# Two input transfers on another queue and the first product begun earlier: the window stage of a fused graph-network kernel

## The chip, the cores and the metric

One core of a Trainium2 chip. The time is the device time of one execution in microseconds; the median of the runs is compared.

## What is computed

`x` has 1,024 nodes of 512 values, and 16,384 edges (`src`, `dst`, sorted by `dst`) join them. Four layers follow each other, each ending in `x = layernorm(x + layer(x))`. Only the first matters here:

```python
h = x @ W + b
adj = zeros((N, N)); adj[row, col] = 1; adj[col, row] = 1
adj = adj + eye(N)
adj = adj / maximum(adj.sum(1), 1)
out = dw[0] * h; cur = h
for i in range(3):
    cur = adj @ cur
    out = out + dw[i + 1] * cur
return relu(out)
```

The other three layers are a sum over edges with a linear layer, a mean over edges, and graph attention. They use the same matrix C of edge counts (1,024 x 1,024), which the kernel builds once from the edges.

## The kernel before

**Building C.** The sorted edges are taken in 32 quads of 512 edges. For each quad three engines work together. VectorE (`key_hots`) compares keys with a row of numbers and so makes the one-hots of the destination, for each of 8 blocks of source nodes times a window of destination nodes (3 of them in quad 0, 41 in quad 31, so 24 to 328 columns). The one-hots of the source (`hot_lo`) come from ScalarE for quads 2, 4, ... 14 and most of those from 17 on (`distances`, four squares, then `lo_hots`, one Relu), and from VectorE for the others. TensorE (`quad`) multiplies both, two windows of two matmuls each, into PSUM. VectorE (`add_window`) adds each window into `c32`, the matrix C, which must have been zeroed. VectorE's program runs three quads ahead (`LOOK`), so in iteration q it adds the windows of quad q and makes the one-hots of quad q + 3.

**Preparation.** SyncE issues the transfers, the edges first. VectorE computes keys and bounds; ScalarE copies `f_lo`; TensorE turns `f_lo` and `f_key` into columns. ScalarE zeroes tiles of C, `ZERO_ACT` of the eight in parts, GpSimd those up to `ZERO_POOL`, VectorE the rest. Products of a zero tile (`warm`) stand between TensorE's first steps.

**h.** The product x @ W0 is cut into 32 parts, four for each of 8 tiles of nodes; a part (`h_part`, line 852) is one float32 matmul of 512 columns that the trace records as two. `h_parts(q)` says which parts follow quad q, in proportion to each quad's work, from quad 2 to quad 28. When a tile's four parts are done, ScalarE (`h_upper`) evicts it in two activations and VectorE (`h_lower`) takes the low half. Both stand in the engines' programs a fixed number of quads behind `h_quad(t)`, the quad after which tile t is complete. Ahead of the third tile's first part TensorE waits for `far_in`, a flag that VectorE reads in iteration 7 from the PSUM bank that this tile will write.

**Order by hand.** Each engine's program is a fixed sequence; semaphores join them. TensorE waits for W0 and the first piece of x after quad 2. Behind the last quad come the turned blocks of C (line 928) and the adjacency products (lines 976, 991, 1001, 1010), and the other layers.

Of the kernel before, what the change touches and what calls it, by code (L numbers as in the profile page):

```python
# [26 lines left out]
P = 128  # L27
# [18 lines left out]
KEYS = NT * (NQ - 1 + (NQ - 1) // 4 + WIN0)  # L46
RING = 5
LOOK = 3
H_FROM = 2
H_TO = 29  # L50
LO_TURN = 16
WARM = (9, 3, 6, 3)
FILL_FROM, FILL = 29, (1, 6)
COLUMNS_AT = {28: (0,), 29: (1,), 30: (2,)}
H_BANKS = (2, 3, 4, 5, 2, 3, 4, 5)
XT_NODES = ((0, P), (P, HALF), (HALF, N))
ZERO_ACT, ZERO_POOL = 5, 6
F_LO_AFTER = 2
KEYS0 = 144
LEFT_GROUP = 48  # L60
# [48 lines left out]
def window(q):  # L109
    return q + q // 4 + WIN0  # L110
# [6 lines left out]
def build(nc, x, xT, src, dst, W0, b0, dw, W1T, b1, wc, wn, b2, W3, W3T, b3, b3T, aw, ab, out):  # L117
    with ExitStack() as ctx:
# [174 lines left out]
        def by_chunk(t):  # L293
            return t.rearrange("p (c g) -> p g c", c=NC)
# [11 lines left out]
            return H_BANKS[t]  # L306

        def h_parts(q):
            def upto(i):
                return NT * KT * sum(27 + window(j) for j in range(H_FROM, i)) // sum(  # L310
                    27 + window(j) for j in range(H_FROM, H_TO))

            return range(upto(q), upto(q + 1)) if H_FROM <= q < H_TO else ()

        def h_quad(t):
            return min(q for q in range(NQ) if KT * t + KT - 1 in h_parts(q))
# [9 lines left out]
        @block.sync  # L326
        def _(sp):
            sp.dma_start(e_dst, dst.rearrange("(g e) -> g e", e=GROUP)).then_inc(S["edges"], 16)
            sp.dma_start(e_src, src.rearrange("(g e) -> g e", e=GROUP)).then_inc(S["edges"], 16)
            sp.dma_start(first_i[:, 0, :], dst.rearrange("(a g e) -> a g e", a=1, e=GROUP)[:, :, 0],  # L330
                         allow_slow_non_contiguous=True).then_inc(S["edges"], 16)
            sp.dma_start(dwb[:], dw.rearrange("(a d) -> a d", a=1).broadcast_to([P, STEPS + 1])).then_inc(S["dw_in"], 16)
            sp.dma_start(w0raw, W0.rearrange("(k p) n -> p k n", p=P)).then_inc(S["w_in0"], 16)
            for i, (n0, n1) in enumerate(XT_NODES):
                sp.dma_start(xT32[:, :, n0:n1], xT.rearrange("(k p) n -> p k n", p=P)[:, :, n0:n1]).then_inc(S[f"xT_in{i}"], 16)
            sp.dma_start(w3t, W3T.rearrange("(k p) n -> p k n", p=P)).then_inc(S["w_in5"], 16)
            sp.dma_start(xcur[:], x.rearrange("(t p) d -> p t d", p=P)).then_inc(S["x_in"], 16)
            sp.dma_start(b0w, b0.rearrange("(a d) -> a d", a=1).broadcast_to([P, D])).then_inc(S["small_in"], 16)
            for i, b in enumerate((b1, b2, b3)):
                sp.dma_start(bb[:, i, :], b.rearrange("(a d) -> a d", a=1).broadcast_to([P, D])).then_inc(S["small_in"], 16)  # L340
            sp.dma_start(wbc[:], b3T).then_inc(S["small_in"], 16)
            sp.dma_start(abb[:], ab.rearrange("(a h) -> a h", a=1).broadcast_to([P, H])).then_inc(S["small_in"], 16)
            sp.dma_start(abc[:], ab.rearrange("(h a) -> h a", a=1)).then_inc(S["small_in"], 16)

            sp.wait_ge(S["const_ready"], 5)
            step = VCOL + H + 2
            flat = abT[:].rearrange("p k c -> p (k c)")
            for q in range(2):
                for u in range(2):
                    c0 = VCOL * u + q  # L350
                    sp.dma_start(flat[q * DH:(q + 1) * DH, c0:c0 + 3 * step + 1:step],
                                 aw.rearrange("(j q) (u p) -> q u p j", q=2, p=DH)[q, u],
                                 allow_slow_non_contiguous=True).then_inc(S["small_in"], 16)

            sp.wait_ge(S["h_done"], NT)
            for n, w in enumerate((W1T, wc, wn, W3)):
                if n >= 2:
                    sp.wait_ge(S["w_lo"], n - 1)
                sp.dma_start(stage[:, n % 2], w.rearrange("(k p) n -> p k n", p=P)).then_inc(S[f"w_in{n + 1}"], 16)
            for layer in range(1, 3):  # L360
                for t in range(NT):
                    name = ("xT_even", "xT_odd")[t % 2]
                    n = (layer - 1) * NT + t
                    sp.wait_ge(S["x_lo"], layer * NT + t + 1)
                    if n >= 2:
                        sp.wait_ge(S[name], n // 2 * TURNED)
                    for v in range(2):
                        sp.dma_start(xTs[:, v, :, t * P:(t + 1) * P], cur[:, 1, v, t, :],
                                     transpose=True).then_inc(S[name], 16)
            sp.wait_ge(S["uT_in"], 1)  # L370
            sp.dma_start(u_rows.rearrange("h (t p) -> (h t) p", p=P), uT).then_inc(S["u_kept"], 16)
            sp.wait_ge(S["u_kept"], 16)
            sp.wait_ge(S["wx_done"], NT)
            for h in range(2):
                sp.dma_start(uf[:, h], u_rows[h:h + 1].broadcast_to([P, N])).then_inc(S[f"uf_in{h}"], 16)
            for t in OUT_ORDER:
                if t in NORM_ACT:
                    sp.wait_ge(S["out_act"], NORM_ACT.index(t) + 1)
                else:
                    sp.wait_ge(S["out_dve"], NORM_DVE.index(t) + 1)  # L380
                sp.dma_start(out.rearrange("(t p) d -> t p d", p=P)[t], xcur[:, t, :]).then_inc(S["out_done"], 16)
            sp.wait_ge(S["out_done"], 16 * NT)
# [99 lines left out]
        def _(act):  # L482
            def copy(o, i, scale=1.0, **kw):
                return act.activation(o, i, ACT.Copy, scale=scale, **kw)  # L484

            act.sem_inc(S["wx_in"], 2)
            act.sem_inc(S["nv_in"], 2)
            act.wait_ge(S["cols"], 3)
# [5 lines left out]
            zeros(0, F_LO_AFTER)  # L494
            act.wait_ge(S["prep"], LO_IN)
            copy(f_lo, i_lo).then_inc(S["f_lo_in"], 1)
            zeros(F_LO_AFTER, 2 * F_LO_AFTER)

            def split_hi(n, name, raw):
                act.wait_ge(S[f"w_in{n}"], 16)  # L500
# [2 lines left out]
                copy(ws[:, SLOT[name], 0], raw).then_inc(S["w_hi"], 1)  # L503

            act.wait_ge(S["tr"], 1)
            act.activation(lo16[:], by_chunk(ps[:, 2, 0:E // P]), ACT.Copy, bias=1.0).then_inc(S["nslo_in"], 1)
            copy(nslo[:], by_chunk(ps[:, 2, 0:E // P]), -1.0).then_inc(S["nslo_in"], 1)
            act.wait_ge(S["nslo_in"], 2)
            act.wait_ge(S["const_ready"], 4)
            mine = [q for q in range(NQ) if lo_by_act(q)]  # L510
# [18 lines left out]
                copy(cur[:, 0, 0, t, :], ps[:, h_bank(t), :]).then_inc(S["h_hi"], 1)  # L529
                copy(acc[:, t, :], ps[:, h_bank(t), :], dwb[:, 0:1]).then_inc(S["acc0"], 1)  # L530

            def constants():

                for k0, k1 in ((KEYS0, 2 * KEYS0), (2 * KEYS0, KEYS)):
                    act.activation(iota_rep[:, k0:k1, :], iota_rep[:, 0:k1 - k0, :], ACT.Copy, bias=float(k0)).then_inc(S["keys_late"], 1)
                copy(id16[:], id32[:]).then_inc(S["const16"], 1)
                copy(sel[:], id32[0:H, 0:H + 1].unsqueeze(2).broadcast_to([H, H + 1, P])).then_inc(S["const16"], 1)

            tiles_up = 0
            act.wait_ge(S["dw_in"], 16)  # L540
            distances(0)
            zeros(2 * F_LO_AFTER, ZERO_ACT)
            for i, q in enumerate(mine):
                if i + 1 < len(mine):
                    distances(i + 1)
                lo_hots(i)
                if i == 2:
                    constants()
                if mine[i - 1] <= FAR_QUAD < q:
                    act.wait_ge(S["tr"], 3)  # L550
                    act.activation(far, by_chunk(ps[:, 5, 0:E // P]), ACT.Copy, bias=-1.0).then_inc(S["far_in"], 1)
# [3 lines left out]

            for t in range(tiles_up, NT - 1):
                h_upper(t)

            def cast_left(j):
                copy(cst[:, j:j + 2, 0:HALF], c32[:, j:j + 2, 0:HALF]).then_inc(S["cst_left"], 1)  # L560
# [232 lines left out]
        def _(pe):  # L793
# [21 lines left out]
            def warm(n):  # L815

                for _ in range(n):
                    mm(ps[:, 4, :], blank[:, 0:P], blank, start=True, stop=True)

            pe.wait_ge(S["blank_in"], 1)  # L820
            warm(WARM[0])
            pe.wait_ge(S["const_ready"], 4)
            pe.wait_ge(S["f_lo_in"], 1)
            for c in range(NC):
                ins = pe.transpose(ps[:, 2, c * NG:(c + 1) * NG], f_lo[:, c * P:(c + 1) * P], id32[0:NG, 0:NG])
            ins.then_inc(S["tr"], 1)
            warm(WARM[1])
            pe.wait_ge(S["prep"], F_KEY_IN)
            for c in range(NC):
                ins = pe.transpose(ps[:, 3, c * NG:(c + 1) * NG], f_key[:, c * P:(c + 1) * P], id32[0:NG, 0:NG])  # L830
            ins.then_inc(S["tr"], 1)
            warm(WARM[2])

# [44 lines left out]
                        fill(FILL[0])  # L878

            def far_columns():  # L880
                pe.wait_ge(S["idx_far"], 2)
                for c in range(NC):
                    pe.transpose(ps[:, 5, c * NG:(c + 1) * NG], f_far[:, c * P:(c + 1) * P], id32[0:NG, 0:NG])
# [14 lines left out]
            def attention_bias():  # L898
# [4 lines left out]
                ins = mm(ps[:, 3, 264:264 + H], one[:].broadcast_to([P, P]), wba[:, 0, :], start=True, stop=True)  # L903
                ins.then_inc(S["wa_done"], 1)

            for q in range(NQ):
                if q == FILL_FROM:
                    pe.wait_ge(S["acc0"], 5)
                    pe.wait_ge(S["h_lo"], 5)
                quad(q)  # L910
                if q < H_FROM:
                    warm(WARM[3])
                if q == H_FROM:
                    pe.wait_ge(S["key_in"], 1)
                    pe.wait_ge(S["nslo_in"], 2)
                    pe.wait_ge(S["xT_in0"], 16)
                    pe.wait_ge(S["w_in0"], 16)
                if q == FAR_QUAD:
                    far_columns()
                for n in h_parts(q):  # L920
# [362 lines left out]
        def _(dve):  # L1283
# [45 lines left out]
            dve.wait_ge(S["first_in"], 3)  # L1329
            tt(pack, pack, trio[:, :, 1], ALU.bitwise_or).then_inc(S["first_in"], 1)  # L1330
            dve.wait_ge(S["tr"], 2)
            dve.tensor_copy(key16[:], by_chunk(ps[:, 3, 0:E // P])).then_inc(S["key_in"], 1)
            dve.wait_ge(S["first_in"], 5)
            ts(pack, pack, 10, None, ALU.logical_shift_left).then_inc(S["first_in"], 1)
            dve.wait_ge(S["const_ready"], 4)
# [43 lines left out]
            key_hots(1, 1)  # L1379
            lo_hots(1)  # L1380
            key_hots(2, 0)
            dve.wait_ge(S["c32z"], 5)
            tiles_low = 0
            key_hots(2, 1)
            for q in range(NQ):
# [536 lines left out]
```

## Time and profile before

| | |
|---|---|
| median of 3 runs | 385.77 us (385.58 to 386.03) |
| the profiled execution | 385.64 us |
| its span, first to last instruction | 383.8 us |
| TensorE's mean granted clock in it | 0.989 of full |
| TensorE busy | 369.2 us |
| VectorE busy | 277.8 us |
| ScalarE busy | 235.4 us |
| GpSimd busy | 100.3 us |

The first three rows tell how a time read from the trace stands to the measured ones: the span leaves out 1.84 us of its own execution. Busy times are sums over the whole span and overlap.

### The profile page before, as it was taken

To read this page: it belongs to the slowest core of one execution; us is meant where nothing else is said; L and a number is where in the kernel's file an instruction comes from. 1 tells how busy PE (TensorE), PEld (TensorE's weight loads), DVE (VectorE), ACT (ScalarE), POOL (GpSimd) and SP (SyncE) were. 2 spreads that over 40 slices of the span, in tenths; PEclk is the share of its full clock that TensorE was granted. 3 is DMA by queue.
4 is the path that set the end of the run, shared out by engine and by line. 5 is a ranking of instruction groups with operands and counts; after the bars stand their busy time and mean duration, and the time that the engine had idled before them with its cause. 6 is when DMAs were issued, how large, how long until landed. Compare 5 with 4: busy or idle time off the path is not lost.

```text
span 383.8 us, 7745 instructions
## 1 busy us (share of the span) xinstructions
PE 369.2 (96%) x2740; PEld 217.3 (57%) x2740; DVE 277.8 (72%) x608; ACT 235.4 (61%) x402; POOL 100.3 (26%) x91
## 2 busy tenths in 40 slices
PE   8799999999999999999999999999999999999980
PEld 3355585444444444444444444444568889999980
DVE  8799988469986772226755445553995979999994
ACT  8999866678512444222651111477877999999234
POOL 3003000098700477000990000466300000121210
PEclk9999999999999999999999999999999999999995
DMA  5970060032000000000442000133203113110005
GB/s 163 385 236 0 3 207 14 2 127 92 2 0 0 1 2 3 0 2 1 86 94 41 0 0 2 27 80 73 41 2 115 56 55 113 56 57 3 2 3 222
DMA packets 27974, 22.70 MB, mean 59 GB/s; under 512 B 19552, under 2 KB 20768, under 8 KB 27936
## 3 DMA queue, kind: packets, MB, share of 16 engines
q1 hardware_dynamic: 27072, 19.06, 16.9%
q10 hardware_dynamic: 864, 3.15, 2.3%
q8 instruction: 23, 0.38, 0.4%
q14 instruction: 15, 0.12, 0.1%
HBM read 15.87 MB, written 2.13 MB: 47 GB/s over the span
## 4 chain that ended last, share of the span: by engine, by line
PE 87%; DVE 5%; ACT 5%; issue 2%; DVEq 0%; POOL 0%; POOLq 0%
PE ps L805 22%; PE ps L1205 10%; PE ps L1146 8%; PE ps L1047 7%; PE ps L1088 7%; PE ps L1010 7%; PE ps L1001 7%; PE ps L852 6%; PE ps L976 4%; PE ps L991 4%; PE ps L873 3%; ACT cts L516 2%; DVE early L1775 1%; ACT xcur L727 1%; PE ps L893 1%
## 5 line engine op out<-in xcount | busy, mean ns | idle before, releaser
L805 PE MATMUL ps<-big,xTs 128*128 128x512 f16 x384 | 84.3, 379 | 0.0
L805 PEld LDWEIGHTS ps<-big,xTs 128*128 128x128 f16 (+1 forms) x384 | 37.0, 98 | 43.5
L713 ACT ACTIVATE big<-big,uvt 128x1024 bf16<-128x1024 f32 x55 | 58.8, 1147 | 0.0
L614 ACT ACTIVATE big<-xcur,nmr,rstd (+1 forms) x24 | 19.5, 814 | 33.9 <-DVE nmr L1491 33.9
L445 POOL TENSOR_TENSOR big<-xcur,big x16 | 18.5, 1156 | 60.2 <-ACT xcur L615 59.2
L852 PE MATMUL ps<-big,xTs 128*128 128x512 f32 x64 | 32.6, 606 | 0.0
L462 POOL TENSOR_TENSOR xcur<-xcur,c 128x512 f32<-128x512 f32 (+2 forms) x8 | 8.8, 1104 | 87.7 <-DVE c L1694 83.1
L484 ACT ACTIVATE big<-ps 128x512 f16<-128x512 f32 (+1 forms) x16 | 9.4, 587 | 33.3 <-PE ps L805 30.9
L1146 PE MATMUL ps<-big,cst 128*128 128x260 f16 x256 | 29.8, 275 | 0.0
L415 POOL TENSOR_TENSOR big<-xTs,big 128x2048 f16<-128x2048 f32 x4 | 16.2, 4080 | 44.8 <-ACT big L484 44.8
L1010 PE MATMUL ps<-big,adj 128*128 128x512 f16 x128 | 27.9, 379 | 0.0
L1047 PE MATMUL ps<-cst,big 128*128 128x512 f16 x128 | 27.8, 379 | 0.1
L1001 PE MATMUL ps<-big,adj 128*128 128x512 f16 x128 | 27.8, 379 | 0.0
L1088 PE MATMUL ps<-big,cts 128*128 128x512 f16 x128 | 27.8, 379 | 0.0
L1146 PEld LDWEIGHTS ps<-big,cst 128*128 128x128 f16 x256 | 24.3, 96 | 4.8
L1361 DVE TENSOR_TENSOR c<-c,ps 128x24 f32 (+31 forms) x64 | 21.3, 333 | 3.3 <-PE ps L873 3.1
L453 POOL TENSOR_TENSOR big<-xcur,big 128x512 f16<-128x512 f32 x8 | 9.3, 1158 | 51.9 <-ACT xcur L615 51.9
L1344 DVE TENSOR_TENSOR adj<-adj,early 128x48 f16<-128x48 f16 (+31 forms) x64 | 21.7, 341 | 0.4 <-issue 0.2
L873 PEld LDWEIGHTS ps<-adj,cts 128*128 128x128 f16 x128 | 11.1, 107 | 18.2 <-issue 12.1
L1047 PEld LDWEIGHTS ps<-cst,big 128*128 128x128 f16 x128 | 12.4, 98 | 15.4 <-issue 0.6
L1088 PEld LDWEIGHTS ps<-big,cts 128*128 (+1 forms) x128 | 12.5, 98 | 15.1
L1001 PEld LDWEIGHTS ps<-big,adj 128*128 128x128 f16 x128 | 12.5, 98 | 15.1
(226 smaller groups left out, 713.8 us busy)
## 6 DMA issues: line engine op xcount, KB each, us to landing
big<-u_rows ACTq DMA_DIRECT2D x6, 512.0 KB, 3.7
xcur<-in_x SPq DMA_DIRECT2D x1, 2048.0 KB, 17.2
out<-xcur SPq DMA_DIRECT2D x8, 256.0 KB, 2.3
big<-in_W SPq DMA_DIRECT2D x1, 1024.0 KB, 6.0
xTs<-in_xT SPq DMA_DIRECT2D x1, 1024.0 KB, 10.1
big<-in_W3T SPq DMA_DIRECT2D x1, 1024.0 KB, 12.9
xTs<-in_W1T SPq DMA_DIRECT2D x1, 1024.0 KB, 5.5
xTs<-in_wc SPq DMA_DIRECT2D x1, 1024.0 KB, 8.3
```

The source lines that it names most:

```text
L713: act.activation(above[:, a % AHEAD, :], uf[:, h % 2], ACT.Relu, scale=BIG, bias=vb[:, j, h:h + 1]).then_inc(S["above_in"], 1)
L805: return mm(bank, lhs(k)[a], rhs(k)[b], start=start and k == 0 and n == 0, stop=stop and k == KT - 1 and n == 2)
L852: ins = mm(bank, xT32[:, k, t * P:(t + 1) * P], w0raw[:, k, :], start=k == 0, stop=k == KT - 1)
L873: ins = mm(ps[:, WINDOW_BANKS[w % 4], 0:n], left, hot_key[:, r, w % 2 * NC * n:(w % 2 + 1) * NC * n].rearrange("p (k c) -> p k c", c=NC)[: ...
L1001: ins = mm(ps[:, t, :], adj[:, j, t * P:(t + 1) * P], cur[:, 1, v, j, :], start=n == 0 and v == 0, stop=n == NT - 1 and v == 1)
L1010: ins = mm(ps[:, t, :], adj[:, j, bass.ds(t * P, P)], cur[:, 0, v, j, :], start=n == 0 and v == 0, stop=n == NT - 1 and v == 1)
L1047: ins = mm(ps[:, half * KT + k, :], cur[:, 1, v, j, k * P:(k + 1) * P], c[:, j, half * HALF:(half + 1) * HALF], start=c is cst and j == 0 ...
L1088: ins = mm(ps[:, t, :], c[:, j, bass.ds(t * P, P)], cur[:, 0, v, j, :], start=c is cts and j == 0 and v == 0, stop=c is parts[-1] and j == ...
L1146: ins = mm(ps[:, DENSE_BANK[i], 0:4 * (DH + 1)], cst[:, j, t * P:(t + 1) * P], yh[:, j, v, 4 * half:4 * half + 4, DH + 1:YW], start=j == 0 ...
L1205: ins = mm(o, cz[h % CZ][:, j, t * P:(t + 1) * P], yh[:, j, v, h, :], start=j == 0 and v == 0, stop=j == NT - 1 and v == 1)
L1344: tt(hot_key[:, q % RING, w * NC * n:(w + 1) * NC * n].rearrange("p (k c) -> p k c", c=NC), iota_rep[:, 0:n, 0:NC], spread(key16[:], q, n) ...
L1361: added = tt(cells, cells, ps[:, WINDOW_BANKS[w % 4], 0:NT * m].rearrange("p (a w) -> p a w", w=m), ALU.add)
```

## The change

- W0 and the first 128 nodes of the turned x are issued by ScalarE, as the first things it does, no longer by SyncE.
- TensorE waits for both ahead of quad 0, and parts 0 and 1 of h stand there; part 2 follows quad 0, part 3 quad 1. The remaining 28 are spread over quads 2 to 28. The warm-up products behind quads 0 and 1 are gone, and those ahead of quad 0 are one instead of six.
- ScalarE zeroes four tiles of C instead of five, GpSimd two instead of one.
- ScalarE makes the one-hot of its first quad straight behind its squares, and fills the late part of `iota_rep` where it did before, but `id16` and `sel` only behind all h tiles save the last.
- The banks of the turned columns move (2 and 3 to 4 and 5), the warm-up's from 4 to 3, and the waits that guarded them move to where the banks are used again.

```diff
-H_FROM = 2
+H_FIRST, H_FROM = {-1: (0, 1), 0: (2,), 1: (3,)}, 2
-WARM = (9, 3, 6, 3)
+WARM = (9, 3, 1)
-ZERO_ACT, ZERO_POOL = 5, 6
+ZERO_ACT, ZERO_POOL = 4, 6
...
         def h_parts(q):
+            if q in H_FIRST:
+                return H_FIRST[q]
...
-                return NT * KT * sum(27 + window(j) for j in range(H_FROM, i)) // sum(
+                return KT + (NT - 1) * KT * sum(27 + window(j) for j in range(H_FROM, i)) // sum(
                     27 + window(j) for j in range(H_FROM, H_TO))
...
-            sp.dma_start(w0raw, W0.rearrange("(k p) n -> p k n", p=P)).then_inc(S["w_in0"], 16)
-            for i, (n0, n1) in enumerate(XT_NODES):
+            for i, (n0, n1) in enumerate(XT_NODES[1:], 1):
...
+            act.dma_start(w0raw, W0.rearrange("(k p) n -> p k n", p=P)).then_inc(S["w_in0"], 16)
+            act.dma_start(xT32[:, :, 0:P], xT.rearrange("(k p) n -> p k n", p=P)[:, :, 0:P]).then_inc(S["xT_in0"], 16)
...
             act.wait_ge(S["dw_in"], 16)
             distances(0)
-            zeros(2 * F_LO_AFTER, ZERO_ACT)
+            lo_hots(0)
+            distances(1)
             for i, q in enumerate(mine):
-                if i + 1 < len(mine):
+                if 0 < i < len(mine) - 1:
                     distances(i + 1)
-                lo_hots(i)
+                if i:
+                    lo_hots(i)
                 if i == 2:
-                    constants()
+                    keys_late()
...
             for t in range(tiles_up, NT - 1):
                 h_upper(t)
+
+            constants()
...
             def far_columns():
+                pe.wait_ge(S["nslo_in"], 2)
+                pe.wait_ge(S["key_in"], 1)
                 pe.wait_ge(S["idx_far"], 2)
...
+            pe.wait_ge(S["w_in0"], 16)
+            pe.wait_ge(S["xT_in0"], 16)
+            for n in h_parts(-1):
+                h_part(0, n)
             for q in range(NQ):
...
                 quad(q)
-                if q < H_FROM:
-                    warm(WARM[3])
-                if q == H_FROM:
-                    pe.wait_ge(S["key_in"], 1)
-                    pe.wait_ge(S["nslo_in"], 2)
-                    pe.wait_ge(S["xT_in0"], 16)
-                    pe.wait_ge(S["w_in0"], 16)
...
-            dve.wait_ge(S["c32z"], 5)
+            dve.wait_ge(S["c32z"], 4)
```

By `h_parts` 8 parts stand ahead of quad 8 after the change and 5 before; h tile 0 is complete behind quad 1 instead of quad 6, tile 2 begins behind quad 8 instead of quad 11.

## Rows read from the trace of the kernel before

**Rows 1.** The page: busy time, share of the span and instructions of each engine.

```profile
PE 369.2 (96%) x2740; PEld 217.3 (57%) x2740; DVE 277.8 (72%) x608; ACT 235.4 (61%) x402; POOL 100.3 (26%) x91
```

**Rows 2.** The chain in order of time: start, length in us, what.

```profile
8.30 0.94 ACT c L484
...
15.40 0.20 ACT id L484
15.60 1.05 ACT sel L484
...
54.77 0.50 DVE c L1361
...
58.02 1.89 PE ps L976 x8
```

**Rows 3.** Busy time by stretch: stretch, its length, then each engine's busy us.

```profile
24.00:50.82 26.82, 26.82 (x119) 14.26 (x117) 26.82 (x81) 24.33 (x60) 3.33 (x5) 1.00 0.07 16
50.82:55.83 5.01, 5.01 (x54) 4.49 (x51) 4.05 (x10) 2.81 (x4) 0.00 (x0) 1.00 0.88 264
```

**Rows 4.** Waits of VectorE from 9.5 to 55.85: total, times, longest.

```profile
DVE c L1361 <- PE ps L873: 3.1, 6, 0.9
```

**Rows 5.** Timeline of SyncE's issues: start, length, line, destination and source.

```profile
3.26 0.43 SPq L333 DMA_DIRECT2D big<-in_W  x1
3.74 1.87 SPq L335 DMA_DIRECT2D xTs<-in_xT  x3
```

**Rows 6.** Transfers: size and us from issue to landing.

```profile
big<-in_W SPq DMA_DIRECT2D x1, 1024.0 KB, 6.0
...
xTs<-in_xT SPq DMA_DIRECT2D x1, 256.0 KB, 6.4
```

**Rows 7.** Transfers from 4 to 5 us, then from 6 to 7 us.

```profile
DMA packets 118, 0.04 MB, mean 38 GB/s; under 512 B 100, under 2 KB 100, under 8 KB 118
...
DMA packets 190, 0.39 MB, mean 389 GB/s; under 512 B 0, under 2 KB 0, under 8 KB 190
```

**Rows 8.** Timeline of ScalarE and GpSimd: start, length, instruction, idle time before.

```profile
0.89 1.28 ACT L484 ACT_TABLE_LOAD   x1 [0.89 <-PEq L1915]
...
4.46 0.42 ACT L484 ACTIVATE cst<-cst 64x256 f32<-64x256 int32 x1 [0.37 <-DVE cst L1309]
...
9.50 0.23 POOL L408 MEMSET abT<- 128x160 f32 x1 [5.31 <-PE ps L873]
...
20.23 0.57 ACT L484 ACTIVATE big<-ps 128x512 f16<-128x512 f32 x1
20.71 0.67 ACT L484 ACTIVATE acc<-ps,dwb 128x512 f32<-128x512 f32 x1
```

**Rows 9.** TensorE: the timeline at quad 8, then two pieces of the chain.

```profile
18.55 0.37 PE L873 MATMUL ps<-adj,cts 128*128 128x104 f16 x4 [0.74 <-ACT cts L524]
...
19.84 0.21 PE ps L873 x4
20.05 0.92 PE ps L852 x2
```

**Rows 10.** Timeline of VectorE: additions of quads 0, 2, 8 and 10, and the flag.

```profile
9.50 0.18 DVE L1361 TENSOR_TENSOR c<-c,ps 128x24 f32 x1
...
11.93 0.20 DVE L1361 TENSOR_TENSOR c<-c,ps 128x40 f32 x1 [0.85 <-PE ps L873]
...
18.03 0.14 DVE L1405 CAST flags<-f_flag 1x1 int32<-1x1 f32 x1
19.12 0.26 DVE L1361 TENSOR_TENSOR c<-c,ps 128x104 f32 x1 [0.94 <-PE ps L873]
...
21.36 0.28 DVE L1361 TENSOR_TENSOR c<-c,ps 128x120 f32 x1 [0.21 <-PE ps L873]
```

**Rows 11.** Later transfers that ScalarE issues: ns of an issue, min, median, max.

```profile
L703 ACTq DMA_DIRECT2D big<-u_rows x6: 326/327/351, 302.0 to 338.5; - x6
```

**Rows 12.** Groups by line and shape, 0 to 56 us: the lower halves of h.

```profile
L1368 DVE TENSOR_TENSOR big<-ps,big 128x512 f16<-128x512 f32 x7 | 4.8, 684 | 0.0
```

More of the change, by code:

```diff
@@ L308, in h_parts @@
         def h_parts(q):
+            if q in H_FIRST:
+                return H_FIRST[q]
             def upto(i):
-                return NT * KT * sum(27 + window(j) for j in range(H_FROM, i)) // sum(
+                return KT + (NT - 1) * KT * sum(27 + window(j) for j in range(H_FROM, i)) // sum(
                     27 + window(j) for j in range(H_FROM, H_TO))
-            return range(upto(q), upto(q + 1)) if H_FROM <= q < H_TO else ()
+            return tuple(range(upto(q), upto(q + 1))) if H_FROM <= q < H_TO else ()
         def h_quad(t):
@@ L496, in _ @@
             copy(f_lo, i_lo).then_inc(S["f_lo_in"], 1)
-            zeros(F_LO_AFTER, 2 * F_LO_AFTER)
+            zeros(F_LO_AFTER, ZERO_ACT)
             def split_hi(n, name, raw):
@@ L505, in _ @@
             act.wait_ge(S["tr"], 1)
-            act.activation(lo16[:], by_chunk(ps[:, 2, 0:E // P]), ACT.Copy, bias=1.0).then_inc(S["nslo_in"], 1)
-            copy(nslo[:], by_chunk(ps[:, 2, 0:E // P]), -1.0).then_inc(S["nslo_in"], 1)
+            act.activation(lo16[:], by_chunk(ps[:, 4, 0:E // P]), ACT.Copy, bias=1.0).then_inc(S["nslo_in"], 1)
+            copy(nslo[:], by_chunk(ps[:, 4, 0:E // P]), -1.0).then_inc(S["nslo_in"], 1)
             act.wait_ge(S["nslo_in"], 2)
@@ L530, in h_upper, with keys_late, constants @@
                 copy(acc[:, t, :], ps[:, h_bank(t), :], dwb[:, 0:1]).then_inc(S["acc0"], 1)
-            def constants():
+            def keys_late():
                 for k0, k1 in ((KEYS0, 2 * KEYS0), (2 * KEYS0, KEYS)):
                     act.activation(iota_rep[:, k0:k1, :], iota_rep[:, 0:k1 - k0, :], ACT.Copy, bias=float(k0)).then_inc(S["keys_late"], 1)
+            def constants():
                 copy(id16[:], id32[:]).then_inc(S["const16"], 1)
@@ L817, in warm @@
                 for _ in range(n):
-                    mm(ps[:, 4, :], blank[:, 0:P], blank, start=True, stop=True)
+                    mm(ps[:, 3, :], blank[:, 0:P], blank, start=True, stop=True)
             pe.wait_ge(S["blank_in"], 1)
@@ L824, in _ @@
             for c in range(NC):
-                ins = pe.transpose(ps[:, 2, c * NG:(c + 1) * NG], f_lo[:, c * P:(c + 1) * P], id32[0:NG, 0:NG])
+                ins = pe.transpose(ps[:, 4, c * NG:(c + 1) * NG], f_lo[:, c * P:(c + 1) * P], id32[0:NG, 0:NG])
             ins.then_inc(S["tr"], 1)
@@ L829, in _ @@
             for c in range(NC):
-                ins = pe.transpose(ps[:, 3, c * NG:(c + 1) * NG], f_key[:, c * P:(c + 1) * P], id32[0:NG, 0:NG])
+                ins = pe.transpose(ps[:, 5, c * NG:(c + 1) * NG], f_key[:, c * P:(c + 1) * P], id32[0:NG, 0:NG])
             ins.then_inc(S["tr"], 1)
@@ L1331, in _ @@
             dve.wait_ge(S["tr"], 2)
-            dve.tensor_copy(key16[:], by_chunk(ps[:, 3, 0:E // P])).then_inc(S["key_in"], 1)
+            dve.tensor_copy(key16[:], by_chunk(ps[:, 5, 0:E // P])).then_inc(S["key_in"], 1)
             dve.wait_ge(S["first_in"], 5)
```

## The prediction

> **What bounds the kernel now.** I read the page first: TensorE is busy for nearly the whole span [rows 1]. An average says nothing about one stage, so I went on to the chain of waits in order of time. The change touches only the first 58 us. The chain there has three parts. Up to 18.55 it runs along ScalarE: its tail is the copy that fills `sel`, and then the one-hot of quad 8, for which TensorE waits [rows 2, 9]. From 18.55 to 54.77 it is printed as TensorE. At 54.77 it goes to VectorE (last addition of a window), and at 58.02 TensorE begins with the adjacency products, which it then runs without a pause that matters [rows 2].
>
> The second part must not be taken at its word. The busy time by stretch shows VectorE at 26.82 of 26.82 us between 24.00 and 50.82, the same as TensorE [rows 3]. All that VectorE waited for TensorE after its first addition is 3.1 us in six waits [rows 4]. So the window stage has two bounds of one size. Work taken off TensorE after 18.55 buys at most the part of those 3.1 us that lies there. The first question is therefore when VectorE's run of additions begins, and which of its waits remain.
>
> **Which quantity decides.** Before, quad 0 needs nothing from memory but the edges. After, TensorE waits ahead of quad 0 for W0 and for the first 128 nodes of x transposed (256 KB), then does parts 0 and 1 of h. I call the moment when TensorE can begin part 0 L, and write everything else as L plus something.
>
> **The change part by part.**
>
> *The two transfers.* Before, SyncE issues W0 as its fifth transfer, at 3.26, and the piece of x at 3.74, since each issue takes it about 0.5 to 0.6 us [rows 5]. They land 6.0 and 6.4 us after issue, at 9.26 and 10.14 [rows 6]. ScalarE can issue at about 0.8, the time at which SyncE's first issue and ScalarE's table load start [rows 5, 8]. With the old 6.0 us W0 lands at 6.8, and x follows by the old distance of 0.9: 7.7. That is the lower bound of L for another reason too: TensorE's own preparation ends there, as shown below. Against it: SyncE now issues the larger pieces of x from 3.26 on, and their bytes run beside the small piece, where before they stood behind it in one queue. At full flow the engines move 389 GB/s, and nearly nothing in the second in which W0 began [rows 7]. By equal bytes the 256 KB take 1.4 to 1.7 us in place of 0.7 to 0.9, and L is 8.5. Packet for packet, 512-byte rows against 1,536-byte rows, the piece gets a quarter of the flow and takes 2.7 to 3.4 us: L is 10.1. In W0's favour: it no longer stands in SyncE's queue behind the small transfers of the edges' first entries and of `dw`, in whose wake only 0.04 MB moved between 4 and 5 us [rows 7]. I take L = 8.3, near the equal-byte value, and keep 7.7 and 10.1 as the ends.
>
> The Trainium skill, "DMA: Bandwidth & Descriptors", section "Issuing engines are not separate DMA queues", speaks against this edit: transfers from different issuing engines share the same 16 DMA engines, and a second issuer saves only issue time. Here the issue time saved is itself 2.5 us, so by that rule the edit would still pay if the later pieces stay out of the way; no row of before shows two such queues at once.
>
> *ScalarE's start.* It now issues two transfers before its table load. SyncE took 0.48 and about 0.6 for the same two [rows 5]; ScalarE's own issues later take 0.33 each [rows 11]. So 0.7 to 1.1 us, I take 1.0. Its first zeroing ends at 5.0 instead of 4.0, but it had waited 0.37 us for VectorE there, so the copy of `f_lo` starts 0.5 late, at 5.0 in place of 4.46 [rows 8]. TensorE's two groups of transposes come 0.5 late, and TensorE is ready at about 7.7. VectorE's first one-hots, begun from those, end at 10.0 instead of 9.5, where its first addition stood [rows 10].
>
> *ScalarE up to quad 8.* Removed: the fifth tile of zeros, 0.94 us of the chain, and the copies that fill `id16` and `sel`, 0.20 + 1.05 us [rows 2]: 2.2 us. Added: 0.5 from the start, 0.1 because the one-hot of quad 2 follows its squares directly, and the eviction of h tile 0, now due after quad 4 instead of after quad 10: two activations of 0.57 and 0.67 that overlap their neighbours by about 0.1 each, 1.05 [rows 8]. The hot of quad 8, at 18.5 before, is there at about 18.0 to 18.1 if h tile 0 is in time.
>
> *The zero tile on GpSimd.* Its memset becomes one of two tiles, about 1 us longer; GpSimd stood idle for 5.31 us ahead of its next work at 9.50 [rows 8], and the additions begin no earlier. Nothing waits. The constants behind the h tiles (1.25 us) fall behind the last but one h tile, in the stretch in which ScalarE has no more one-hots to make, well ahead of the turn of C at 54.7; nothing. VectorE's wait on the zeros had been over already.
>
> *TensorE.* On the chain a part of h costs 0.92 us (two matmul records) and an early quad 0.21 [rows 9]. Four parts (3.7 us) move in front of quads 0 to 2, where TensorE had warm-up products and waits; after quad 8 there are 24 parts instead of 27, 2.7 us less. As VectorE is as full there [rows 3], this is worth only its end waits.
>
> *The sum, along VectorE.* Parts 0 and 1: quad 0 starts at L + 1.9. From a quad's start to its first addition pass 0.57 us (18.55 to 19.12) [rows 9, 10]. Quad 1 follows at L + 3.05, quad 2 at L + 4.2, and VectorE's addition of quad 2 at L + 4.75. From there to the flag copy in iteration 7 it needed 6.24 us before (11.93 to 18.17) [rows 10], about 0.2 of it in the sixth wait (3.1 less 0.85, 0.94, 0.21 and the 0.9 behind 50.82 leaves that) [rows 3, 4, 10]; the lower half of h tile 0, now due in iteration 5, adds 0.6 (0.68 less the overlap) [rows 12]. So the flag is there at L + 11.35. This matters: part 8 of h writes the bank that the flag is read from, it now follows quad 8 instead of quad 11, and so waits for the flag. Part 8, quad 9, part 9, quad 10: quad 10 starts at L + 13.4 and is added at L + 13.9. From the addition of quad 10 (21.36) to the end of the last one (55.83) are 34.5 us, of which 0.96 is waiting after 50.82 [rows 3, 10]; less that, and less the 0.6 moved ahead, 32.9. Sum: L + 46.8.
>
> With L = 8.3 the last addition ends at 55.1 instead of 55.83: 0.7 us. TensorE, by the same count, is through its windows 1 to 2 us ahead of before, so VectorE decides. The stages behind 58.02 shift as they are. The profiled execution took 385.64 for a span of 383.8, 1.84 outside it, and the median of the runs is 385.77, 0.13 above it. So 383.1 + 1.84 + 0.13 = 385.1.
>
> **Rivals.** What a measurement of this kernel can tell from no change is about 0.2%, 0.77 us.
>
> 1. *The piece of x comes late (slower).* The queues alternate packet by packet, L = 10.1, end at 56.9: 1.1 us slower, 386.9. For it: SyncE's rows are three times as long, and the flow is already at the limit behind 6 us [rows 7]. Against it: the two transfers start 2.5 us sooner and have the engines to themselves until about 5. It turns slower at L = 9.0, measurably at 9.8. The Trainium skill, same page, section "Queues, rings and completion order", states such an alternation, so by that rule this would be the case. Chance 0.2.
>
> 2. *No contention.* Both have landed by 7.7, and ScalarE's 0.5 us is all that holds the start: end at 54.5, 1.3 faster, 384.5. For it: the window before 5 us in which almost nothing flowed. Chance 0.25.
>
> 3. *TensorE alone is the bound.* Then quad 8 half a microsecond sooner and 2.7 us less work behind it give 3.2: 382.6. The row of 24.00 to 50.82 speaks against it [rows 3]. Chance 0.04.
>
> 4. *Issuing costs ScalarE double,* 2 us, as two engines issue at once. Everything from the transposes on is a further 1.0 late, VectorE is ready at 11.0, which stands for L = 8.55, and the hot of quad 8 comes near 19: end near 55.4 to 55.8, at best 0.4 faster, no change that can be told: 385.6. Chance 0.08.
>
> 5. *The clock.* It is at its upper level throughout [rows 3]. With fewer warm-up products TensorE may idle from 7.7 to L. It idled 0.74 us before 18.55 without falling [rows 9], so only with a late L could it fall; this goes with rival 1.
>
> **How the numbers follow.** The forecast case, L between 7.9 and 9.0, has 0.43, and its own range is 384.7 to 385.8. A little under half of it is beyond 0.77 us. Faster by over 0.2%: 0.2 of the forecast case, 0.25 and 0.04, together 0.49. Slower by over 0.2%: most of rival 1, 0.16. Within: 0.35. The range: at the low end rival 2 with half a microsecond for the terms that I rounded (384.0), at the high end rival 1 (386.9), which leaves about 2 in 10 outside.
>
> **What would show it.** The first h part ahead of quad 0, starting near 8.3; the first addition at 10.8 (L + 2.45) where it was at 9.5; ScalarE's transfers issued from 0.8 and its `f_lo` copy at 5.0; TensorE waiting for VectorE's flag ahead of part 8, near 19.6; VectorE without a wait between 24 and the last addition, which ends near 55.1. If the end of the last addition is not L + 46.8 within 0.5, the sum along VectorE is wrong; if L is not 8.3, the transfers are. A W0 that lands later than 8, or a wait of ScalarE for h tile 0 longer than 1 us, would break it. So would a program that does not have these instructions in this order on ScalarE, transfers first and table load after: with the load (1.28 us [rows 8]) in front, L is above 9 and nothing is gained.

## The result, and the profile after

The changed kernel takes 391.36 us (median of 4 runs, 390.83 to 392.02) against 385.67 of the kernel before on the same chip: ratio 1.0147, 95% interval 1.0135 to 1.0159. It is 5.7 us slower, where 385.1 was forecast, and it lies outside the range. The profiled execution's span is 389.7 us, 5.9 more than before. Lines below the edit stand 10 or 11 higher: h parts L863, quads L884, additions L1371, adjacency products L986 to L1057.

The chain of the kernel after, in order of time: start, length in us, what.

```profile
2.00 6.10 DMA first_i<-in_dst
8.12 0.27 DVE base L1318
...
9.18 0.45 PE ps L836 x2
...
11.97 2.37 PE ps L863 x4
14.34 0.12 PE ps L884 x4
...
58.97 0.51 DVE c L1371
...
61.70 1.89 PE ps L986 x8
147.08 0.48 issue
147.56 1.46 PE ps L1057 x6
149.02 1.83 issue
150.85 26.50 PE ps L1057 x122
```

Two losses make up the difference. The first lies ahead of 14 us: the chain now begins with a transfer of 0.2 KB that takes 6.10 us, and all behind it is late. The last addition ends at 59.48 (58.97 + 0.51) where it ended at 55.83 [rows 3], and L986 starts 3.7 us later than its like in [rows 2]. The second lies at 147: TensorE does six products of the third adjacency group and then nothing for 1.83 us, with no engine that it waits for. From 61.70 to 147.08 are 85.4 us, as many as before (58.02 to 143.41); there the third group followed as one piece:

```profile
143.41 0.11 issue
143.52 27.79 PE ps L1047 x128
```

The transfers of the kernel after, 0 to 12 us: size, us from issue to landing.

```profile
big<-in_W ACTq DMA_DIRECT2D x1, 1024.0 KB, 6.1
...
xTs<-in_xT ACTq DMA_DIRECT2D x1, 256.0 KB, 6.7
...
cst<-in_dst SPq DMA_DIRECT2D x1, 64.0 KB, 5.2
cst<-in_src SPq DMA_DIRECT2D x1, 64.0 KB, 6.0
first_i<-in_dst SPq DMA_DIRECT2D x1, 0.2 KB, 6.1
```

ScalarE and VectorE of the kernel after: start, length, instruction, idle time before.

```profile
0.74 0.47 ACTq L488 DMA_DIRECT2D big<-in_W  x1
1.23 0.53 ACTq L489 DMA_DIRECT2D xTs<-in_xT  x1
1.94 1.28 ACT L486 ACT_TABLE_LOAD   x1 [1.94 <-issue]
...
8.12 0.27 DVE L1318 TENSOR_SCALAR base<-cst,top,low 64x1 f32<-64x1 int32 x1 [3.93 <-DMA first_i<-in_dst]
```

The two transfers do what was foreseen: W0 has landed at 6.84 (0.74 + 6.1) and the piece of x at 7.93 (1.23 + 6.7). The edges don't. Before, they took 2.4, 2.2 and 1.9 us; now 5.2, 6.0 and 6.1, so VectorE's first step on the edges (L1318) comes at 8.12 in place of 4.12. The queues in three successive microseconds of the kernel after (2 to 3, 3 to 4, 4 to 5 us) show why. q10 is ScalarE's queue, q1 SyncE's; behind each stand its packets, MB and share of the time of the 16 DMA engines. What the profile calls a packet is one row of a transfer here, 2 KB of W0 or 1 KB of the edges.

```profile
q10 hardware_dynamic: 65, 0.13, 68.5%
...
q10 hardware_dynamic: 191, 0.39, 101.5%
q1 hardware_dynamic: 3, 0.00, 0.9%
...
q10 hardware_dynamic: 161, 0.33, 90.1%
q1 hardware_dynamic: 74, 0.06, 17.9%
```

Both queues were given their first transfer at 0.74. Up to 4 us, 264 packets of W0 started (8 of them ahead of 2 us) and 3 of SyncE's; before, SyncE's queue moved 259 between 2 and 4 us. 264 packets are 16 to 17 for each of the 16 engines, if they are spread evenly.

### The profile page after: what moved, and what is told of

It is laid out like the page before. It is cut to its first block, busy times and chain, and to the rows that moved or that the text cites. A ratio compares the mean times of both kernels' runs of the same rounds, so it can differ in the third digit from the quotient of the medians.

```text
span 389.7 us, 7722 instructions
## 1 busy us (share of the span) xinstructions
PE 368.8 (95%) x2729; PEld 216.6 (56%) x2729; DVE 277.6 (71%) x608; ACT 234.6 (60%) x401; POOL 100.9 (26%) x91
## 4 chain that ended last, share of the span: by engine, by line
PE 85%; DVE 7%; issue 3%; DMA 2%; ACT 2%; DVEq 1%; SPq 0%
PE ps L816 22%; PE ps L1215 10%; PE ps L1156 8%; PE ps L1057 7%; PE ps L1098 7%; PE ps L1020 7%; PE ps L1011 7%; PE ps L863 5%; PE ps L986 4%; PE ps L1001 4%; PE ps L884 2%; DMA first_i<-in_dst 2%; DVE c L1371 1%; DVE adj L1354 1%; DVE early L1785 1%
## 5 line engine op out<-in xcount | busy, mean ns | idle before, releaser
L863 PE MATMUL ps<-big,xTs 128*128 128x512 f32 x64 | 33.7, 620 | 1.2 <-DVE flags L1415 1.2
L1057 PE MATMUL ps<-cst,big 128*128 128x512 f16 x128 | 28.0, 379 | 2.3 <-issue 2.3
L1371 DVE TENSOR_TENSOR c<-c,ps 128x24 f32 (+31 forms) x64 | 20.8, 325 | 3.1 <-PE ps L884 2.8
L1057 PEld LDWEIGHTS ps<-cst,big 128*128 128x128 f16 x128 | 12.4, 98 | 17.9 <-issue 3.3
L1020 PEld LDWEIGHTS ps<-big,adj 128*128 (+1 forms) x128 | 12.5, 98 | 15.0
```

Source lines behind the costliest of these rows:

```text
L863: ins = mm(bank, xT32[:, k, t * P:(t + 1) * P], w0raw[:, k, :], start=k == 0, stop=k == KT - 1)
L1020: ins = mm(ps[:, t, :], adj[:, j, bass.ds(t * P, P)], cur[:, 0, v, j, :], start=n == 0 and v == 0, stop=n == NT - 1 and v == 1)
L1057: ins = mm(ps[:, half * KT + k, :], cur[:, 1, v, j, k * P:(k + 1) * P], c[:, j, half * HALF:(half + 1) * HALF], start=c is cst and j == 0 ...
L1371: added = tt(cells, cells, ps[:, WINDOW_BANKS[w % 4], 0:NT * m].rearrange("p (a w) -> p a w", w=m), ALU.add)
```

## The experiments

All times are set against the kernel before in the same session, 385.6 to 385.7 us.

**sp_again.** The changed kernel with both transfers back on SyncE.

```diff
-            for i, (n0, n1) in enumerate(XT_NODES[1:], 1):
+            sp.dma_start(w0raw, ...)
+            for i, (n0, n1) in enumerate(XT_NODES):
...
-            act.dma_start(w0raw, ...)
-            act.dma_start(xT32[:, :, 0:P], ...)
```

> The kernel after with W0 and the first piece of x back on SyncE, in their old places; everything else of the change stays. Theory (the edges): the 4 us by which the last edge transfer lands late in the kernel after come from W0's bytes being in flight beside them, so here they land near 4.1 us again and VectorE starts its keys at 4.1. TensorE then waits for the first piece of x until about 10.1, the last window addition ends at 57 to 57.5 us (55.8 before, 59.5 after), and the 1.8 us pause of TensorE inside the aggregate products (line 1057) stays: about 389.4. Rival (ScalarE's program: what costs is h ahead of quad 0 and the new order of the evictions): the time stays at 391.

Measured 390.76 (ratio 1.0143, 1.0124 to 1.0162), 1.4 us above the theory's 389.4 and close to the rival's 391. The edges are on time, as the theory had it, and yet little is won. TensorE can begin h only at 10.28 and stood idle for 2.66 us ahead of it. The busy time by stretch of this kernel (columns as in [rows 3]) shows what followed:

```profile
9.00:10.00 1.00, 0.00 (x0) 0.00 (x0) 0.85 (x5) 0.97 (x4) 0.00 (x0) 1.00 1.10 378
...
11.00:15.00 4.00, 4.00 (x14) 1.50 (x13) 0.93 (x5) 1.58 (x5) 0.34 (x4) 0.57 1.06 386
15.00:16.00 1.00, 1.00 (x10) 0.43 (x9) 0.56 (x4) 0.00 (x0) 0.00 (x0) 1.00 1.05 387
```

The granted clock, 1.00 at 9 to 10, is 0.57 from 11 to 15: for most of it the lower of the two levels. The last addition ends at 58.89, 1.8 later than L + 46.8 gives. The pause is here as well, 1.28 us at 148.47. A third thing came to light, a step of VectorE on the indices that takes 1.01 us; act_only below explains it.

**queue_only**, **w0_only**, **x_only.** The kernel before, with both transfers, with W0 alone, with the x piece alone on ScalarE.

```diff
+            act.dma_start(w0raw, ...)            # not in x_only
+            act.dma_start(xT32[:, :, 0:P], ...)  # not in w0_only
```

> The kernel before with nothing changed but the two transfers, issued by ScalarE. Theory (the edges): the edges land at about 8.1 us instead of 4.1, the whole window stage is 3.5 to 4 us late, no pause in the aggregate products: about 389.5. Rival (only the issue time on ScalarE counts): the zeroing and the f_lo copy come 0.5 us late, 386.3.

> The kernel before, with only the first piece of x (256 KB in rows of 512 bytes) issued by ScalarE; W0 stays on SyncE behind the edges. Theory (each engine serves a run of some 16 packets of one queue before the other's): 16 packets of 27 ns are 0.45 us where W0's are 1.4, and there are only 32 a queue, so the edges land 0.3 to 1 us late, near 4.5 to 5: 385.8 to 386.6. Rival (whatever is queued first goes out whole before the other queue is served): the same 0.9 us at most, as the piece takes 0.9 us alone; what tells them apart is the place of the edges' first packets, ahead of the last of x or behind. Rival (the bytes do not matter, a second queue costs 4 us): 389.5.

> The kernel before with W0 alone issued by ScalarE, as the first thing it does; the 256 KB piece of x stays on SyncE. Theory: it is W0's packets (1 MB, queued from about 0.8) that the edges' packets stand behind, so e_dst, e_src and first_i land 5 to 6 us after issue as with both transfers moved, VectorE's first comparison of indices comes near 8 in place of 4.1, and the time is about that of both moved: 388.5 to 389.5. Rival: the delay needs both transfers in ScalarE's queue (the x piece alone cost half a microsecond): edges 3 to 4 us after issue, 386 to 387.

| | time | ratio (95%) | edges land after | VectorE's first step |
|---|---|---|---|---|
| queue_only | 389.48 | 1.0101 (1.0084 to 1.0118) | 5.0 / 5.9 / 5.9 us | 7.95 |
| w0_only | 388.85 | 1.0084 (1.0067 to 1.0100) | 5.3 / 5.1 / 5.1 us | 7.16 |
| x_only | 386.50 | 1.0018 (1.0008 to 1.0028) | 3.0 / 2.7 / 2.5 us | 4.49 |

All three fell into their expected ranges. The move of the transfers alone costs 3.9 us, and W0 alone 3.2 of them. The x piece delays the edges by about half a microsecond, W0 by 2.9 to 3.2: with one quarter of the bytes about a fifth of the delay. Its rows are 512 bytes, and between 2 and 3 us 490 of its packets went out; so many packets of W0 took until after 5 in the kernel after. These three tell the edges' delay from every other part of the change: nothing else differs in them, and behind SyncE's issues the chain of w0_only begins with it.

```profile
2.00 5.13 DMA first_i<-in_dst
7.16 0.27 DVE base L1308
```

queue_only settles something else as well. TensorE stood idle for 3.80 us there until the edges had come, and from 9 to 15 its granted clock is 0.50, the lower level. Three warm-up products of the kernel after, the same three of queue_only, and queue_only's busy time from 10 to 12:

```profile
9.56 1.46 PE L829 MATMUL ps<-big 128*128 128x512 f16 x3
...
9.39 1.46 PE L819 MATMUL ps<-big 128*128 128x512 f16 x3
...
10.00:12.00 2.00, 2.00 (x7) 0.57 (x5) 1.77 (x12) 1.97 (x7) 0.00 (x0) 0.50 1.05 394
```

The kernel after stood idle for 3.97 us and has the same length, 1.46, where warm_more below has 0.82 at the upper level. The view prints 1.00 for the clock of the kernel after at that time, but its trace holds no record of the clock ahead of 13.15 us, and w0_only's, with three such products of 1.46 as well, none ahead of 13.13. So the lengths speak for the lower level in the first products of the kernel after, and no record speaks against it.

**gated.** The changed kernel, ScalarE waiting for the edges before it issues.

```diff
+            act.wait_ge(S["edges"], 48)
             act.dma_start(w0raw, ...)
```

> The kernel after, with ScalarE waiting until the edges have landed before it issues W0 and the first piece of x. Theory (bursts of one queue): the small transfers on SyncE are late only because W0's packets are already queued on the same 16 engines; without them they land near 4.1 us, though W0 still comes from ScalarE. W0 is then issued near 4.1 beside the later pieces of x, the first piece lands near 11 to 12 us, TensorE idles some 4 us, its granted clock falls to half for about 4 us, and the pause in the aggregate products stays: 391 to 393, no better than after. Rival (a second issuer as such is slow): the edges land at 8 us again.

Measured 399.45 (1.0348, 1.0331 to 1.0365). The rival is out, since the edges are on time (2.3, 2.2, 2.2), but the expected time, 391 to 393, is missed by 6 us: it let the x piece land at 11 to 12. ScalarE issues at 4.18 and 4.72, behind SyncE's larger pieces of x, and now its own transfers are the ones held up. The transfers of this kernel, in us from issue to landing:

```profile
xTs<-in_xT SPq DMA_DIRECT2D x1, 1024.0 KB, 8.6
big<-in_W ACTq DMA_DIRECT2D x1, 1024.0 KB, 11.7
...
xTs<-in_xT ACTq DMA_DIRECT2D x1, 256.0 KB, 14.8
```

W0 takes 11.7 us in place of 6.0 and the 256 KB 14.8 in place of 6.4 [rows 6]; from 4.7 to 9 us 39 packets of ScalarE's queue went out and 862 of SyncE's. TensorE begins h at 19.68, with the granted clock at 0.50. In both orders the queue whose packets were at the engines first held up the other.

**warm_more.** The changed kernel with 20 warm-up products in place of 9 ahead of TensorE's first transposes, so that it has as many as before.

```diff
-WARM = (9, 3, 1)
+WARM = (20, 3, 1)
```

> The kernel after with 11 more warm-up products ahead of its first transposes, where TensorE waits 4 us for the edges, so that its program is as long as before from there on. Theory (where TensorE's code lies): the pause of 1.8 us in the aggregate products, which the trace puts down to no other engine, comes from fetching instructions and moves with the length of the code ahead of it; it goes, and the products of h ahead of quad 0 run faster, since TensorE does not idle: 388.7 to 389.2. Rival (the pause is a wait for data of the first layer norm, which runs as late as the rest): 390.5 to 391.4, the pause stays.

Measured 387.76 (1.0066, 1.0042 to 1.0089), 3.6 us faster than the changed kernel and 0.9 faster than the theory's range. The edges are as late (5.1, 6.2, 6.1). Its chain:

```profile
11.00 1.72 PE ps L863 x4
...
57.24 0.51 DVE c L1371
...
145.35 0.48 issue
145.83 27.79 PE ps L1057 x128
```

TensorE's first h product starts at 10.84 by the timeline (11.00 on the chain), 0.9 sooner, because its products before it run at the upper level's length: three warm-ups take 0.82 us and not 1.46. Parts 0 and 1 then take 1.88 us by the timeline and not 2.58. The last addition ends at 57.75, 1.7 sooner. And the pause is gone: the third group runs as one piece of 27.79, where 1.46 + 1.83 + 26.50 = 29.79 stood. 1.7 and 2.0 are the 3.7 by which the spans differ (386.0 and 389.7).

**warm_fewer.** The kernel before with the 11 products taken out that the change takes out, and nothing else.

```diff
-WARM = (9, 3, 6, 3)
+WARM = (9, 3, 1, 0)
```

> The kernel before with 11 warm-up products fewer (one ahead of quad 0 in place of six, none behind quads 0 and 1), which are the ones that the change takes away; nothing else differs. Theory: TensorE's program is shorter by these instructions, and with that alone it pauses for 1.3 to 2.2 us in the third group of adjacency products, near 143 to 150 us, with no engine that it waits for; the last addition of the window stage ends near 55.8 as before: 387.0 to 387.9. Rival: the pause comes from the late start or from the order of the transfers and not from the length: no pause, 385.7. A second rival: TensorE stands idle ahead of quad 0 without these products and the granted clock falls to half for a while: then the last addition ends one or two us later, with or without a pause.

Measured 388.51 (1.0076, 1.0060 to 1.0093), 0.6 us above the theory's range. The theory's pause is there, and the second rival's fall of the clock as well. The stretches 9 to 10 and 11 to 12 us of this kernel, then its chain:

```profile
9.00:10.00 1.00, 0.31 (x4) 0.21 (x4) 0.78 (x6) 1.00 (x4) 0.34 (x4) 0.87 1.10 376
...
11.00:12.00 1.00, 0.89 (x9) 0.79 (x10) 0.13 (x2) 1.00 (x4) 0.00 (x0) 0.50 1.05 378
```

```profile
59.03 1.89 PE ps L976 x8
...
144.55 1.45 PE ps L1047 x6
146.01 1.91 issue
147.92 26.50 PE ps L1047 x122
```

TensorE, busy for 0.3 us in each of the two microseconds from 8 to 10, falls to a granted clock of 0.50; the window stage ends 1.0 late (59.03 for 58.02). The pause of 1.91 stands behind the sixth product of the third group, the very place of the kernel after. So the pause needs neither the moved transfers nor h ahead of quad 0: taking 11 products out of TensorE's program is enough. Four kernels have it, always behind the sixth product: the changed one, sp_again, gated and this. All four have the 11 products fewer. Of the instruction queue q8 the traces of these four show 24 packets in all, and those of the nine without the pause, the kernel before among them, 23. From 140 to 155 us of this kernel q8 has 3, before it had 2:

```profile
q8 instruction: 3, 0.05, 1.5%
```

The 23 packets of before hold 0.38 MB, 16 to 17 KB each on average, so the engines' programs come in pieces. That TensorE lacks its instructions there while a piece is fetched, and that the 11 products shift where a piece ends, fits these rows but is not shown: no row names a releaser, and q8 is not told apart by engine.

**act_only.** The kernel before with ScalarE's part of the change alone: four tiles zeroed and GpSimd's two, the first one-hot behind its squares, `id16` and `sel` behind the h tiles.

```diff
-ZERO_ACT, ZERO_POOL = 5, 6
+ZERO_ACT, ZERO_POOL = 4, 6
...
-            zeros(2 * F_LO_AFTER, ZERO_ACT)
+            lo_hots(0)
+            distances(1)
```

> The kernel before with only ScalarE's part of the change: four zero tiles, the one-hot of quad 2 behind its squares, id16 and sel behind the h tiles; GpSimd zeroes two tiles. Theory: the one-hot of quad 8 is there at about 16.4 us instead of 18.5; VectorE's waits at quads 8 and 10 (0.94 and 0.21) go, and VectorE is then full to the end: 0.8 to 1.2 us faster, 384.6 to 385. Rival (TensorE alone is the bound of the stage, with 5 parts of h ahead of quad 8): quad 8 starts 0.9 us sooner and everything with it, 384.8 too, but VectorE keeps its waits behind 50.8; or nothing, 385.7, if the window stage is bound by neither.

Measured 384.89 (0.9981, 0.9970 to 0.9993), inside the theory's range: a gain, small. VectorE and GpSimd from 3 to 6 us show what takes part of it back:

```profile
3.25 1.79 POOL L401 MEMSET c<- 128x2048 f32 x1
4.12 0.10 DVE L1315 TENSOR_SCALAR base<-cst,top,low 64x1 f32<-64x1 int32 x1
4.16 1.04 DVE L1316 TENSOR_SCALAR cst<-cst 64x256 int32<-64x256 int32 x1
```

The second step on the indices, which took 0.28 before, takes 1.04; it ends at 5.20, 0.16 after GpSimd's memset (5.04). In sp_again and gated it begins at 4.18 and 4.38 beside the same memset and ends at 5.19 and 5.20. Before, a memset of one tile was over at 4.19.

**zero_later** and **zero_first.** act_only, with GpSimd's second tile behind VectorE's keys, or with both tiles ahead of its iota.

```diff
-            pool.memset(c32[:, ZERO_ACT:ZERO_POOL, :], 0.0)
+            pool.memset(c32[:, ZERO_ACT + 1:ZERO_POOL, :], 0.0)
+            pool.wait_ge(S["prep"], F_KEY_IN)
+            pool.memset(c32[:, ZERO_ACT:ZERO_ACT + 1, :], 0.0)
```

> act_only (the kernel before with ScalarE's part of the change), but GpSimd zeroes its second tile only after VectorE's keys are made. Theory (GpSimd's longer memset holds VectorE up: the operation at 4.18 us took 1.01 us instead of 0.28 beside it): that operation takes 0.28 again, the first additions come 0.5 to 0.7 us sooner than in act_only, 384.2 to 384.5, unless the later memset (0.9 us, near 6.3) holds up another one by as much: then 384.9 as in act_only, with the long operation in another place.

> act_only, with GpSimd's two zero tiles ahead of its number row (iota) instead of behind it, so that they are done before the edges land. Theory as for zero_later: VectorE's operations behind 4.1 us at their old lengths if the iota holds nothing up, first addition near 9.7: 384.2 to 384.5. Rival (the iota, 1.3 us, holds VectorE up as the memset did): the operation at 4.2 is long again, 384.9.

zero_later: 384.01 (0.9954, 0.9938 to 0.9971), the fastest version of the study, 1.7 us under the kernel before and 0.2 faster than expected. zero_first: 384.38 (0.9964, 0.9950 to 0.9978), in the theory's range, though the rival's long step is there. In zero_later the step is short again:

```profile
3.25 0.94 POOL L401 MEMSET c<- 128x1024 f32 x1
4.12 0.10 DVE L1317 TENSOR_SCALAR base<-cst,top,low 64x1 f32<-64x1 int32 x1
4.15 0.27 DVE L1318 TENSOR_SCALAR cst<-cst 64x256 int32<-64x256 int32 x1
```

In zero_first it takes 0.73 beside an iota (3.48 to 4.79) and ends at 4.94, 0.15 after that. The Trainium skill, "SBUF — State Buffer", section "SBUF: two separate sides", says that GpSimd and VectorE, the latter in those of its modes that use two ports, share one pair of ports as an exclusive lock, and that the one that comes second waits for the other's whole instruction; ends 0.15 and 0.16 behind GpSimd's agree with it. No run shows in which mode VectorE's step ran.

**h_ahead.** The changed kernel without its three side costs: transfers on SyncE, 20 warm-ups, GpSimd as in zero_later. Against zero_later only h ahead of quad 0, with its banks and warm-ups, is left.

> The changed kernel freed of its three side costs: both transfers back on SyncE, 11 warm-up products more ahead of the wait for W0, and GpSimd's second tile of zeros behind VectorE's keys. What stays is ScalarE's part and h ahead of quad 0. Theory (the prediction's own sum along VectorE, last addition at L + 46.8, with L now set by SyncE's transfers): TensorE begins h near 10.1 to 10.3, the last addition ends at 56.9 to 57.1 against 55.8 before, no pause in the third group of adjacency products: 386.7 to 387.0, that is 2.7 to 3.0 us slower than the same ScalarE part with h begun behind quad 2. Rival: beginning h ahead of quad 0 is not itself a loss, since work is only reordered: as fast as the ScalarE part alone, 384.0 to 384.9.

Measured 387.28 (1.0045, 1.0028 to 1.0063), 0.3 us above the theory's range; the rival is out. The x piece lands at 10.13, h begins, and the chain reads:

```profile
3.74 6.39 DMA xTs<-in_xT
...
10.27 1.95 PE ps L864 x4
...
56.70 0.51 DVE c L1372
```

10.27 + 46.8 is 57.1; the last addition ends at 57.21. There is no pause. With the transfers on SyncE, to begin with h is 3.3 us slower than to begin with quad 0 (zero_later), which needs no more than the edges.

## Why the prediction was wrong

**The step that failed: "TensorE is ready at about 7.7".** L was to be the later of two moments, the transfers' and TensorE's own. The transfers' moment was right (7.93, inside 7.7 to 8.5). TensorE was ready at 11.76. Its readiness hangs on `f_lo`, this on the edges, and their landing was carried over from before without a word: the last of them landed at 8.10 (2.00 + 6.10) in place of 3.9; the text asked what SyncE's pieces do to ScalarE's, and never what W0's 1 MB does to SyncE's first 128 KB. Of the 4.1 us between 7.7 and 11.76 the late edges alone make 3.1: in warm_more the edges are as late, the products run at the upper level's length, and TensorE is ready at 10.84. The other 0.9 are the long products behind TensorE's 3.97 us of idleness, which the late edges brought too: queue_only and w0_only have them with no product taken out. Parts 0 and 1 took longer as well (2.58 by the timeline for 1.9). With 11.76 the sum gives 58.6; measured 59.5, of which the longer parts are 0.7.

The Trainium skill was read too narrowly here. "DMA: Bandwidth & Descriptors", section "Queues, rings and completion order", says that an engine drains a whole packet of about 9 to 17 descriptors from one ring before it turns to the next; I took it as a turn for each row. W0's rows agree with it, if one row is one descriptor: up to 4 us 221 of them in queue_only and 269 in w0_only had started and none of SyncE's, 14 to 17 for each engine on average. The x piece in x_only does not: up to 2.5 us 314 of its 512-byte rows had started and none of SyncE's, about 20 for each engine. So that a run of some 16 rows sets the delay is not shown; no run varied the row's size of one and the same transfer.

**"The stages behind 58.02 shift as they are": false by 2.4 us.** They shift unchanged up to 147; then come 2.0 us of pause and 0.4 of a longer start (0.48 for 0.11), which warm_more has as well. Fewer warm-up products were costed at nothing because they lie in idle time. They have two prices: a place in the program (warm_fewer: 1.9) and, where TensorE then idles, the clock (warm_fewer: 1.0; sp_again: 1.8). The second depends on what stands behind it: queue_only ran at 0.50 from 9 to 15 too, and its last addition ends 4.1 late (59.91) where VectorE's first step is 3.8 late.

**The clock, tied to a late L alone: too narrow.** It fell after idle time ahead of quad 0 of other causes as well: in queue_only after 3.80 us of waiting for the edges, and in warm_fewer, whose order has no L. In sp_again it fell after 2.66 us of waiting for the x piece, which is the case that was foreseen.

**GpSimd's zero tile, "Nothing waits": false by 0.75 us.** No instruction waits for the memset, but a step of VectorE runs beside it and becomes 1.04 for 0.28. Worth 0.9 us of time (act_only to zero_later, 384.89 to 384.01). In the kernel after it cost nothing: there the step begins at 8.31, long after the memset, and takes 0.28, so it is no part of the 5.7 us.

**The sum along VectorE, L + 46.8: right.** warm_more 10.84 to 57.75 (46.9), h_ahead 10.27 to 57.21 (46.9), and the wait of TensorE for VectorE's flag stands ahead of part 8 as foretold (1.2 us). The kernel after ends at L + 47.7, 0.9 off, most of it in parts 0 and 1. That TensorE alone does not decide (rival 3) was right too: behind 24 us VectorE waited 0.7 us for TensorE in the kernel after, and the count along VectorE holds in the two kernels above.

**ScalarE: right in its price.** Its two issues made the table load 1.05 us later (1.94 for 0.89) where 1.0 was taken, so rival 4 is out. Its copy of `f_lo` came at 8.62 and not at 5.0, since that too waited for the edges. Its edits alone, with GpSimd's second tile put later (zero_later), gain 1.7 us, more than the whole change was to bring.

**Rivals 1 and 2** spoke of a late or early x piece; it came at the value between them. The outcome took the side of rival 1 by a mechanism that no rival had. Nor was the gain of h ahead of quad 0 read against the best order without it: by the sum, h ahead of quad 0 pays over zero_later (54.21) only with L below 7.4, and TensorE's own preparation ends at 7.7 in the forecast.

**The account.** Of the 3.65 us at the end of the last addition, L + 46.8 gives 1.8 with L = 10.84 and 0.9 more with 11.76, the slow parts 0.7; 0.2 is not placed. With the 2.4 behind 147 this is the span's 5.9 (6.05 at the end of the third group; 0.1 comes back later). The parts don't add up singly: with the transfers back (sp_again) only 0.6 is won, since then TensorE waits for the x piece until 10.28, the clock falls, and the pause stays.

**Open.** How two queues share an engine: the counts of rows above fit no one number. What ends a fetched piece of program where it does, and so how the pause could be foreseen from the code; only fewer and more warm-up products were tried.

## What to carry to other kernels

Before a large transfer is given to a second queue, list the small transfers in the first that it will meet in the engines, and who waits for them: the bytes that are wanted first must be ahead in the engines, not only in their own queue. Filler products are not free to remove: look at the granted clock behind the gap, at the length of equal products where no clock is on record, and at "issue" gaps on TensorE far away from the edit. And test an edit of several parts part by part: ScalarE's part of this one gains 0.7 us alone (act_only) and 1.7 with one GpSimd memset put later, under a loss of 5.7.

## What the runs showed of the hardware

- A 0.2 KB transfer took 6.1 us when a 1 MB transfer had been issued on another queue 1.3 us before it, and 1.9 without.
- A 256 KB transfer took 3.1 us on ScalarE's queue ahead of all others (x_only), 6.4 on SyncE's behind W0, and 14.8 on ScalarE's behind W0 and beside 4.0 MB that SyncE's queue moved meanwhile (gated).
- VectorE's 64x256 int32 operation took 0.28 us alone, 1.04 beside a GpSimd memset and 0.73 beside an iota, and ended 0.15 to 0.16 after them.
- TensorE paused for 1.83 us (the kernel after), 1.91 (warm_fewer), 1.28 (sp_again) and 1.28 (gated) in the middle of equal products, with one more instruction packet in the trace, and not at all with 11 products more.
- TensorE's products behind 3 to 4 us of idleness had the length of the lower level (three of 128x512: 1.46 us, not 0.82), in traces with a record of the clock at 0.50 (queue_only) and in traces without a record there (the kernel after, w0_only).
